# The mixture of a decoder layer: all experts on all tokens, or tokens scattered by expert through DRAM and gathered back

## The chip, the core and the metric

The kernel runs on one core of one Trainium2 chip. The metric is the device time of one execution in microseconds (us), median of several runs. The core's engines are TensorE (PE in the rows, with PEld for its weight loads), VectorE (DVE), ScalarE (ACT), GpSimd (POOL) and SyncE (SP). Sixteen DMA engines serve it.

## What is computed

Two decoder layers over x of 16 sequences, 128 tokens and 256 features, all in fp32. Each of the six sub-blocks is x + f(layernorm(x)): a recurrence, a grouped attention with a context, **the feed-forward block with a mixture of experts** (the one that is changed), a windowed attention, a cross attention and a gated feed-forward block. The changed block, shortened:

```python
dense_in = rms(h, pre1)
dense_out = rms(gelu(dense_in @ w_gate) * (dense_in @ w_up) @ w_down, post1)     # 256 -> 1024 -> 256
probs = softmax((rms(h) * router_scale * ROOT) @ router_w)                        # 8 experts
top_w, top_i = top_k(probs, 2);  top_w = top_w / sum(top_w) * per_expert_scale[top_i]
aff = zeros(T, 8).at[arange(T), top_i].set(top_w)
g, u = moe_in @ we_gate[e], moe_in @ we_up[e]                                     # moe_in = rms(h, pre2), 256 -> 128
eo = (gelu(g) * u) @ we_down[e]                                                   # 128 -> 256
moe_out = rms(sum_e(aff[e] * eo[e]), post2)
x = x + rms(dense_out + moe_out, post)
```

Each token uses 2 of 8 experts; the other six have the weight 0.

## The kernel before

The program is a row of stages, each a block in which the five engines run their own lists of instructions and meet others by semaphores; a stage begins when all engines have left the one before. `experts` (L1022) is the third stage. A `batch` below is one sequence (128 tokens on 128 partitions), a `group` is four batches (512 tokens); there are four groups.

In before, a group goes through 16 steps q. Steps 0 to 7 are slices of 128 of the dense block's 1024 hidden features, steps 8 to 15 the eight experts, each for all 512 tokens. `gate_up(g, q)` (L1177) makes two products of 512 columns, each from three terms (high*high, low*high, high*low, since a number is split into a rounded high part and a rest), 12 matmuls in all. ScalarE takes the gelu (L1245), VectorE multiplies by the other product (`hide`, L1322), ScalarE rounds the result (L1249), VectorE takes the rest (`split_hidden`, L1328), and `down(g, q)` (L1197) makes 12 matmuls of 256 columns. TensorE's order is gate_up(q), down(q-1). For an expert, `weigh` (L1355, L1357) adds its product times its share to `ex_mixture`, four instructions for four batches. `ex_share` is 0 where the token does not use the expert.

At a group's head TensorE transposes four batches (`turn`, L1152), ScalarE copies them to `ex_h_t` and rounds them to `ex_h_high`, and `route` (L1160) makes the router's logits. VectorE finds the two best experts by comparing all pairs (`choose`). During the first group ScalarE rounds all weights and GpSimd takes their rests (L1134), three tiles for each step.

After the last matmul of a group follows the tail: `square` (L1236, ScalarE) and `normalise` (L1125 and L1126, GpSimd, a power of -1/2) for each of three rms norms, and on VectorE `combine` (L1368, L1372), `scale_sum` and `add_sum` (L1379, L1386) and `measure` (L1393, the statistics of the next layernorm). In before the tails of groups 0 to 2 lie beside the steps of the next group; that of the last group has nothing beside it. GpSimd and SyncE do little in the stage; SyncE loads the next stage's four weights (5 MB) at its start. `split_keys`, `set_keys` and `fetch_keys` belong to the stage before and are not changed.

## Time and profile before

| | us |
|---|---|
| median of 3 runs | 1542.45 (1539.98 to 1542.99) |
| the profiled execution's own time | 1544.03 |
| its span in the trace | 1542.2 |
| `experts`: first matmul of group 0 | 368.73 |
| first matmul of groups 1, 2, 3 | 442.93, 515.21, 586.19 |
| last matmul ends | 656.77 |
| the next stage's first VectorE instruction | 673.64 |

Over the span PE is busy 1336.0 us (87%), PEld 1047.2, DVE 1066.6, ACT 838.5 and POOL 596.0. A timeline line says start, duration, engine, line, operation, output and inputs, count, and in brackets how long the engine sat idle before and what released it. A matmul's duration overlaps that of the next, so that the pace is read from the starts. A matmul of two fp32 operands (the router's) stands as two passes in the trace: 16 rows for 8 instructions.

### The profile page before, as it was taken

To read this page: it belongs to the slowest core of one execution; us is meant where nothing else is said; L and a number is where in the kernel's file an instruction comes from. 1 tells how busy PE (TensorE), PEld (TensorE's weight loads), DVE (VectorE), ACT (ScalarE), POOL (GpSimd) and SP (SyncE) were. 2 spreads that over 40 slices of the span, in tenths; PEclk is the share of its full clock that TensorE was granted. 3 is DMA by queue.
4 is the path that set the end of the run, shared out by engine and by line. 5 is a ranking of instruction groups with operands and counts; after the bars stand their busy time and mean duration, and the time that the engine had idled before them with its cause. 6 is when DMAs were issued, how large, how long until landed. Compare 5 with 4: busy or idle time off the path is not lost. (4 is left out here: it accounts for less than half of the span.)

```text
span 1542.2 us, 26692 instructions
## 1 busy us (share of the span) xinstructions
PE 1336.0 (87%) x8144; PEld 1047.2 (68%) x8144; DVE 1066.6 (69%) x2067; ACT 838.5 (54%) x1853; POOL 596.0 (39%) x685
## 2 busy tenths in 40 slices
PE   6994888886999999928998999899987899888998
PEld 5772555555888888816776777777766565557887
DVE  6997888893566676677777777877784566653443
ACT  5452888884543434345665666566654456552332
POOL 2003655555610000047656656656664333310000
PEclk9996999997999999968999999999999799998999
DMA  8001333313000000020000000000000000000000
GB/s 311 3 0 40 84 82 82 82 42 136 1 1 1 0 0 1 1 99 1 1 1 0 0 0 0 0 0 0 0 1 2 4 4 3 3 1 0 15 14 28
DMA packets 30739, 40.28 MB, mean 26 GB/s; under 512 B 4369, under 2 KB 25873, under 8 KB 29265
## 3 DMA queue, kind: packets, MB, share of 16 engines
q1 hardware_dynamic: 30672, 39.45, 8.4%
q8 instruction: 35, 0.57, 0.2%
q14 instruction: 32, 0.25, 0.1%
HBM read 28.96 MB, written 2.10 MB: 20 GB/s over the span
## 5 line engine op out<-in xcount | busy, mean ns | idle before, releaser
L1811 ACT ACTIVATE wi_weights<-wi_psum,wi_bias,wi_scale 128x128 f32<-128x128 f32 x256 | 113.9, 454 | 114.4 <-DVE wi_bias L1921 114.4
L1586 POOL TENSOR_TENSOR wi_straight<-wi_straight,wi_crossed 128x512 f32<-128x512 f32 x80 | 109.9, 1373 | 5.8 <-DVE wi_crossed L1907 5.7
L951 DVE TENSOR_REDUCE gq_top<-gq_psum 128x4 f32<-128x512 f32 x128 | 86.8, 678 | 28.6 <-PE gq_psum L838 27.8
L1574 POOL TENSOR_TENSOR wi_scratch<-wi_sums,wi_eps 128x4 f32<-128x4 f32 x80 | 36.2, 452 | 161.3 <-DVE wi_sums L1890 159.9
L1912 DVE TENSOR_REDUCE wi_top<-wi_psum 128x4 f32<-128x512 f32 x64 | 44.0, 688 | 75.6 <-PE wi_psum L1701 75.5
L905 ACT ACTIVATE gq_weights<-gq_weights 128x512 f32<-128x512 f32 x128 | 81.3, 635 | 22.0 <-DVE gq_weights L959 20.6
L845 PE MATMUL gq_psum<-const,gq_weights 128*128 128x128 f32 x512 | 79.2, 278 | 15.0 <-ACT gq_weights_t L911 15.0
L1125 POOL TENSOR_TENSOR ex_scratch<-ex_squares,ex_eps 128x4 f32<-128x4 f32 x12 | 2.4, 201 | 229.6 <-ACT ex_junk L1236 229.6
L1249 ACT ACTIVATE ex_hidden_high<-ex_gated 128x512 fp32r<-128x512 f32 x64 | 40.5, 633 | 92.5 <-DVE ex_gated L1322 92.5
L1322 DVE TENSOR_TENSOR ex_gated<-ex_gated,ex_psum 128x512 f32<-128x512 f32 x64 | 43.9, 686 | 64.0 <-PE ex_psum L1177 52.6
L959 DVE TENSOR_TENSOR gq_weights<-gq_psum,gq_top 128x512 f32<-128x512 f32 x128 | 87.2, 681 | 0.0
L1575 POOL TENSOR_TENSOR wi_scale<-wi_scratch,minus_half 128x4 f32<-128x4 f32 x80 | 84.6, 1057 | 6.3
L1652 PEld LDWEIGHTS wi_psum<-const,wi_straight 128*128 128x128 f32 x320 | 51.1, 174 | 50.9 <-issue 50.0
L911 ACT ACTIVATE gq_weights_t<-gq_psum 128x512 f32<-128x512 f32 x128 | 76.0, 594 | 11.8 <-PE gq_psum L845 11.0
L845 PEld LDWEIGHTS gq_psum<-const,gq_weights 128*128 128x128 f32 x512 | 62.1, 142 | 29.8 <-ACT gq_weights_t L911 16.9
L1723 PE MATMUL wi_psum<-wi_wo_high,wi_out_high 128*128 128x256 f32 x256 | 46.0, 302 | 41.7 <-DVE wi_out_low L1875 39.1
L1710 PE MATMUL wi_psum<-wi_weights_t,wi_values 128*128 128x512 f32 x128 | 78.3, 697 | 0.8 <-DVE wi_weights_t L1928 0.8
L1907 DVE TENSOR_TENSOR wi_crossed<-wi_raw,wi_sin_q 128x256 f32<-128x256 f32 x128 | 78.8, 655 | 0.0
L2335 DVE TENSOR_REDUCE cr_top<-cr_psum 128x4 f32<-128x512 f32 x64 | 43.7, 682 | 45.8 <-PE cr_psum L2150 45.8
L1245 ACT ACTIVATE ex_gated<-ex_psum 128x512 f32<-128x512 f32 x64 | 38.1, 596 | 64.0 <-PE ex_psum L1177 64.0
L1596 POOL TENSOR_TENSOR wi_weights<-wi_weights,wi_inverse 128x512 f32<-128x512 f32 x64 | 66.4, 1038 | 8.9 <-remote 4.6
L1701 PEld LDWEIGHTS wi_psum<-wi_k_t,wi_q_t 128*128 128x128 f32 x512 | 68.4, 194 | 1.7
(343 smaller groups left out, 4078.3 us busy)
## 6 DMA issues: line engine op xcount, KB each, us to landing
gq_keys<-in_ctx_keys_dram SPq DMA_DIRECT2D x16, 512.0 KB, 3.8
gq_keys_diagonal<-gq_key_parts SPq DMA_DIRECT2D x64, 128.0 KB, 3.9
x<-in_x_dram SPq DMA_DIRECT2D x4, 512.0 KB, 8.6
gate<-in_gate_dram SPq DMA_DIRECT2D x2, 1024.0 KB, 5.7
up<-in_up_dram SPq DMA_DIRECT2D x2, 1024.0 KB, 7.7
down<-in_down_dram SPq DMA_DIRECT2D x2, 1024.0 KB, 9.9
wq<-in_wq_dram SPq DMA_DIRECT2D x1, 2048.0 KB, 9.9
wo<-in_wo_dram SPq DMA_DIRECT2D x1, 2048.0 KB, 14.3
```

Source lines behind the costliest of these rows:

```text
L845: mm = pe.transpose(ps[:, bank(unit, t, u), j * P:j * P + P], weights[:, u % RINGS, j * P:j * P + P], ident)
L905: act.activation(weights[:, u % RINGS], weights[:, u % RINGS], ACT.Exp, scale=SCALE).then_inc(weighed, 1)
L911: act.activation(weights_t[:, u % PTS], ps[:, bank(unit, t, u), :], ACT.Copy).then_inc(taken, 1)
L951: dve.tensor_reduce(top[:, u % 4, :], rows(u), AX.X, ALU.max).then_inc(topped, 1)
L959: dve.tensor_tensor(weights[:, u % RINGS].rearrange("p (j t) -> p j t", t=P), rows(u), wide(top[:, u % 4, :], [P, 4, P]), ALU.subtract).th ...
L1575: found = pool.tensor_tensor(scale[:, scale_at], scratch2[:], net.half[:, 0:4], ALU.pow)
L1586: added_up = pool.tensor_tensor(straight[:, at], straight[:, at], crossed[:, at], ALU.add)
L1596: pool.tensor_tensor(weights[:, g % 2], weights[:, g % 2], wide(inverse[:, g % 2], [P, 4, P]), ALU.mult).then_inc(normalised, 1)
L1701: mm = pe.matmul(bank[:, j * P:j * P + P], q_t[:, g % 2, j, :], k_t[:, s, g, :], start=False, stop=(j == 3), skip_group_check=True)
L1710: pe.matmul(ps[:, AV, :], values[:, s, g * DH:g * DH + DH], weights_t[:, g % 2], start=True, stop=True).then_inc(attended, 1)
L1811: act.activation(weights[:, g % 2, j, :], ps[:, SC + g % 2, j * P:j * P + P], ACT.Exp, bias=bias[:, g % 2, j:j + 1], scale=scale[:, g, j:j ...
L1907: dve.tensor_tensor(crossed[:, at, :, to], raw[:, at, :, source], over_heads(sin[:, to]), ALU.mult).then_inc(parts, 1)
```

## The change

1. **The experts leave the steps.** STEPS is 8 instead of 16; a group is now only the dense block. Its result is copied out of PSUM to `ex_dense`, which now holds all 16 batches.
2. **The router is brought forward.** All 16 batches are normalised at once into `ex_y`. Batches 4 to 15 are transposed and routed in four rounds of three batches, between steps 1 to 4 of group 0. VectorE chooses for all 16 batches at once in steps 5 to 7.
3. **Places are counted.** With three small matmuls (`count`) and a scan, each (token, expert) pair gets a place in a list that is sorted by expert, each expert padded to whole blocks of 128 places. 2 x 16 x 128 pairs need at most 40 blocks (`TILES`). Indices are whole numbers in `ex_index`; `ex_owner` says whose each block is.
4. **Scatter.** GpSimd issues 32 indirect DMAs, each 128 rows of 1 KB of `ex_y` to their places in `slot_x` in DRAM. `slot_x` is cleared by one DMA of 5.2 MB in the first stage.
5. **Mixture.** Behind three dense groups (`EARLY`), 20 pairs of blocks run: SyncE fetches a pair (256 KB, 4 buffers), TensorE makes 4 transposes, loads the owners of both blocks into registers, makes 12 matmuls of 256 columns with weights addressed by these registers (gate and up side by side in one tile `egu`), 2 transposes and 6 matmuls of 256 columns; SyncE stores the pair to `slot_y` (3 buffers). All 40 blocks are always run.
6. **Gather and tail.** When all pairs are stored, GpSimd issues 32 indirect DMAs that bring back two rows for each token (`ex_first`, `ex_second`). The fourth dense group runs meanwhile, with group 0's tail in its steps 4 to 7. The tails of groups 1, 2 and 3 follow the last matmul.
7. The load of the next stage's weights is issued behind all stores. Expert weights are rounded in group 1 by ScalarE and their rests taken in group 2 by VectorE.

The core of the diff:

```diff
@block.sync
+            def fetch(k):
+                if k >= XINS:
+                    sp.wait_ge(s_turned, k - XINS + 1)
+                sp.dma_start(slot_rows[:, k % XINS], slot_block(net.slot_x, k)).then_inc(slots_in[k % XINS], 16)
+            def store(k):
+                sp.wait_ge(s_taken, k + 1)
+                sp.dma_start(slot_block(net.slot_y, k), s_out[:, k % OUTS]).then_inc(stored[k % OUTS], 16)
+            sp.wait_ge(scattered, 16 * TOP * NB)
+            for k in range(XINS):
+                fetch(k)
+            for k in range(PAIRS):
+                if k + XINS < PAIRS:
+                    fetch(k + XINS)
+                store(k)
...
             load_attn1(nc, net, ("wk", "wv", "wq", "wo"))
@block.gpsimd
+            for i in range(TOP):
+                pool.wait_ge(indexed, i + 1)
+                for b in range(NB):
+                    pool.indirect_dma_start(net.slot_x[:], bass.IndirectOffsetOnAxis(ap=index[i][:, b:b + 1], axis=0),
+                                            y[:, b, :], None).then_inc(scattered, 16)
...
+            gather(0)
+            gather(1)
+            normalise(0, 1)
+            gather(2)
+            gather(3)
+                normalise(0, 2)
+                normalise(3, 0)
...
@block.tensor
+            def mixture():
+                pe.wait_ge(owned, 1)
+                of = {}
+                for i in range(-3, PAIRS):
+                    if i + 3 < PAIRS:
+                        slot_turn(i + 3)
+                        of[i + 3] = [pe.value_load(owner[0:1, 2 * (i + 3) + j:2 * (i + 3) + j + 1],
+                                                   min_val=0, max_val=EXPERTS - 1) for j in range(2)]
+                    if 0 <= i + 2 < PAIRS:
+                        slot_gate_up(i + 2, of[i + 2])
+                    if 0 <= i + 1 < PAIRS:
+                        slot_hidden(i + 1)
+                    if i >= 0:
+                        slot_down(i, of.pop(i))
...
@block.vector
+            for g, k in left():
+                late(g, k)
+            finish(NG - 1)
             measure(NG - 1)
```

TensorE, between the dense steps and the experts: before, an expert's step stands behind the dense ones, 12 matmuls of 512 columns for gate and up and 12 of 256 (the last row is the first of these):

```order
L1177 MATMUL ex_psum<-ex_h_high,ex_egate_high 128x512 [waits ex_w_split,ex_hidden_ready]
L1177 MATMUL ex_psum<-ex_h_high,ex_egate_high 128x512
L1177 MATMUL ex_psum<-ex_h_high,ex_egate_low 128x512 x2
L1177 MATMUL ex_psum<-ex_h_low,ex_egate_high 128x512 x2
L1177 MATMUL ex_psum<-ex_h_high,ex_eup_high 128x512 x2
L1177 MATMUL ex_psum<-ex_h_high,ex_eup_low 128x512 x2
L1177 MATMUL ex_psum<-ex_h_low,ex_eup_high 128x512 x2
L1197 MATMUL ex_psum<-ex_edown_high,ex_hidden_high 128x256 [waits ex_logits_read,ex_high_ready]
```

Now a pair's iteration on TensorE begins so (ISA and REGISTER_ALU are register instructions):

```order
L1339 MATMUL ex_psum<-const,ex_slot_rows 128x128 [waits ex_s_split,ex_slots_in0]
L1339 MATMUL ex_psum<-const,ex_slot_rows 128x128 x3
L1383 TENSOR_LOAD ex_owner
L1383 ISA x2
L1383 TENSOR_LOAD ex_owner
L1383 ISA x2
L1353 ISA [waits ex_s_ready,ex_s_split]
L1353 MATMUL ex_psum<-ex_egu_high,ex_s_high 128x256
L1353 ISA
L1353 MATMUL ex_psum<-ex_egu_high,ex_s_high 128x256
L1353 REGISTER_ALU
L1353 MATMUL ex_psum<-ex_egu_low,ex_s_high 128x256
```

The expert's work moved out of the groups into iterations that start with a fetched tile and two loads to registers. On SyncE, in the middle of the mixture (nothing stood here before):

```order
L1157 DMA ex_slot_rows<-slot_x 128x2x256 [waits ex_s_turned]
L1161 DMA slot_y<-ex_s_out 128x2x256 [waits ex_s_taken]
L1157 DMA ex_slot_rows<-slot_x 128x2x256 [waits ex_s_turned]
L1161 DMA slot_y<-ex_s_out 128x2x256 [waits ex_s_taken]
L1157 DMA ex_slot_rows<-slot_x 128x2x256 [waits ex_s_turned]
```

A fetch now stands behind the store of an earlier pair. On VectorE, from the last product on: before,

```order
L1368 SCALAR_TENSOR_TENSOR ex_mixture<-ex_mixture,ex_norm,rows 128x256 [waits ex_dense_ready,ex_norm_ready]
L1368 SCALAR_TENSOR_TENSOR ex_mixture<-ex_mixture,ex_norm,rows 128x256 x3
L1372 TENSOR_TENSOR ex_mixture<-ex_mixture,ex_dense 128x256 [waits ex_own_dve]
L1372 TENSOR_TENSOR ex_mixture<-ex_mixture,ex_dense 128x256 x3
L1379 SCALAR_TENSOR_TENSOR ex_mixture<-ex_mixture,ex_norm,rows 128x256 [waits ex_norm_ready]
L1379 SCALAR_TENSOR_TENSOR ex_mixture<-ex_mixture,ex_norm,rows 128x256 x3
L1386 TENSOR_TENSOR x<-x,ex_mixture 128x256 [waits ex_own_dve]
L1386 TENSOR_TENSOR x<-x,ex_mixture 128x256 x3
```

and now, the first of three such rounds (for groups 1, 2 and 3):

```order
L1670 SCALAR_TENSOR_TENSOR ex_first<-ex_second,ex_weight,ex_first 128x256 [waits ex_scaled] x4
L1692 SCALAR_TENSOR_TENSOR ex_first<-ex_first,ex_norm,rows 128x256 [waits ex_norm2]
L1692 SCALAR_TENSOR_TENSOR ex_first<-ex_first,ex_norm,rows 128x256 x3
L1696 TENSOR_TENSOR x<-x,ex_first 128x256 [waits ex_own_dve]
L1696 TENSOR_TENSOR x<-x,ex_first 128x256 x3
L1677 SCALAR_TENSOR_TENSOR ex_first<-ex_first,ex_norm,rows 128x256 [waits ex_norm1]
L1677 SCALAR_TENSOR_TENSOR ex_first<-ex_first,ex_norm,rows 128x256 x3
L1686 TENSOR_TENSOR ex_first<-ex_first,ex_dense 128x256 [waits ex_dense_ready,ex_own_dve]
L1686 TENSOR_TENSOR ex_first<-ex_first,ex_dense 128x256 [waits ex_dense_ready] x3
L1701 BN_STATS stats<-x 128x6 [waits ex_own_dve]
L1701 BN_STATS stats<-x 128x6 x3
```

The second wait of that round, `ex_norm2`, is for a power that GpSimd takes behind all 32 gathers.

## Rows read from the trace of the kernel before

**Rows 1.** Busy time in stretches, and granted clock (PEclk)

```profile
core 0: us, PE busy (x) PEld busy (x) DVE busy (x) ACT busy (x) POOL busy (x), PEclk, DMA share, GB/s
200.00:250.00 50.00, 41.27 (x286) 26.88 (x284) 43.96 (x87) 41.91 (x79) 29.22 (x24) 1.00 0.32 80
...
368.70:442.90 74.20, 73.09 (x408) 63.79 (x409) 41.77 (x80) 37.91 (x86) 36.38 (x47) 0.96 0.01 5
442.90:514.00 71.10, 70.36 (x399) 61.50 (x399) 47.76 (x105) 29.97 (x63) 3.63 (x6) 0.98 0.00 1
...
656.80:673.60 16.80, 0.00 (x0) 0.00 (x0) 9.27 (x24) 4.08 (x16) 2.42 (x5) 0.52 0.00 0
```

**Rows 2.** Timeline of TensorE, one dense step, and the first expert's step

```profile
378.30 0.63 PE L1177 MATMUL ex_psum<-ex_h_high,ex_gate_high 128*128 128x512 f32 x2
...
381.05 0.64 PE L1197 MATMUL ex_psum<-ex_down_high,ex_hidden_high 128*128 128x256 f32 x4
...
382.48 0.63 PE L1177 MATMUL ex_psum<-ex_h_high,ex_gate_high 128*128 128x512 f32 x2
...
403.86 0.63 PE L1177 MATMUL ex_psum<-ex_h_high,ex_egate_high 128*128 128x512 f32 x2
```

**Rows 3.** Timeline of TensorE between group 0 and group 1

```profile
437.90 1.04 PE L1152 MATMUL ex_psum<-const,ex_h_tok 128*128 128x128 f32 x8
...
440.42 0.74 PE L1197 MATMUL ex_psum<-ex_edown_high,ex_hidden_low 128*128 128x256 f32 x4 [0.53 <-DVE ex_hidden_low L1328]
441.00 2.08 PE L1160 MATMUL ex_psum<-router_w,ex_h_t 128*128 128x8 f32 x16
442.93 1.20 PE L1177 MATMUL ex_psum<-ex_h_high,ex_gate_high 128*128 128x512 f32 x2
443.93 1.05 PE L1177 MATMUL ex_psum<-ex_h_high,ex_gate_low 128*128 128x512 f32 x2
```

**Rows 4.** Timeline, the tail of the last group and the next stage's start

```profile
656.80 1.66 DVE L1357 SCALAR_TENSOR_TENSOR ex_mixture<-ex_psum,ex_share,ex_mixture 128x256 f32<-128x256 f32 x4 [0.83 <-PE ex_psum L1197]
658.49 0.42 ACT L1236 ACTIVATE ex_junk<-ex_mixture 128x256 f32<-128x256 f32 x1 [4.79 <-DVE ex_mixture L1357]
...
660.12 0.42 ACT L1236 ACTIVATE ex_junk<-ex_mixture 128x256 f32<-128x256 f32 x1
...
660.98 1.01 POOL L1126 TENSOR_TENSOR ex_norm<-ex_scratch,minus_half 128x4 f32<-128x4 f32 x1
662.03 1.67 DVE L1368 SCALAR_TENSOR_TENSOR ex_mixture<-ex_mixture,ex_norm,rows 128x256 f32<-128x256 f32 x4 [3.57 <-POOL ex_norm L1126]
663.74 1.43 DVE L1372 TENSOR_TENSOR ex_mixture<-ex_mixture,ex_dense 128x256 f32<-128x256 f32 x4
...
671.91 1.41 DVE L1393 BATCH_NORM_STATS2 stats<-x 128x6 f32<-128x256 f32 x4
...
673.64 1.17 DVE L192 BATCH_NORM_AGGREGATE mean_var<-stats 128x2 f32<-128x6 f32 x16 [0.33 <-PEq L1034]
```

**Rows 5.** DMA issues (count, KB, us to landing); an issue in SyncE's timeline

```profile
out_dram<-x SPq DMA_DIRECT2D x4, 512.0 KB, 3.0
...
xwq<-in_xwq_dram SPq DMA_DIRECT2D x1, 256.0 KB, 2.9
...
675.20 0.43 SPq L186 DMA_DIRECT2D gate<-in_gate_dram  x1
```

**Rows 6.** Idle time of TensorE before line L838, in a loop (us, times)

```profile
its engine sat idle before it (us, times) until:
  issue: 14.9, 17
```

**Rows 7.** Timeline of ScalarE and of GpSimd, one line each

```profile
375.59 0.40 ACT L1228 ACTIVATE ex_gate_high<-gate 128x256 fp32r<-128x256 f32 x1
...
675.21 3.80 POOL L198 TENSOR_TENSOR rstd<-wi_scratch,minus_half 128x15 f32<-128x15 f32 x1
```

More of the change, by code:

```diff
@@ L23 @@
 F32R = mybir.dt.float32r
+I32 = mybir.dt.int32
 P = 128
@@ L1205, in one @@
+            turn(0)
+            route(0)
+            for g in range(NG):
+                if g == EARLY:
+                    mixture()
                 for q in range(STEPS):
+                    if g == 0 and 1 <= q <= 4:
+                        turn_ahead(q)
+                    if g == 1 and q == 1:
+                        count()
                     gate_up(g, q)
+                    if g == 0 and 1 <= q <= 4:
+                        route(q)
                     if q > 0:
                         down(g, q - 1)
-                if not last:
+                if g + 1 < NG:
@@ L1210, in one @@
                     turn(g + 1)
                 down(g, STEPS - 1)
-            turn(0)
-            rounds(pe, one)
         @block.scalar
@@ L1240, in one @@
+            for q in range(2):
+                round_weights(q)
+            take(0)
+            for g in range(NG):
+                if g == EARLY:
+                    square_dense(EARLY - 1)
+                    mixture()
                 for q in range(STEPS):
-                    if first and q + 2 < STEPS:
+                    if g == 0 and q + 2 < STEPS:
                         round_weights(q + 2)
+                    if g == 0 and 1 <= q <= 4:
+                        take_ahead(q)
@@ new lines, in scale_dense, with mix @@
+            def scale_dense(b, source):
+                dve.scalar_tensor_tensor(dense[:, b, :], source, norm[:, 0, b:b + 1], row("L0_ffn_rn_post1"),
+                                         ALU.mult, ALU.mult).then_inc(dense_ready, 1)
+            def mix(g):
+                for b in range(GB * g, GB * g + GB):
+                    dve.wait_ge(scaled, b + 1)
+                    dve.scalar_tensor_tensor(first[:, b, :], second[:, b, :], weight[:, 1, b:b + 1], first[:, b, :],
+                                             ALU.mult, ALU.add).then_inc(mixed, 1)
@@ L1380, in scale_sum, with finish @@
+                for b in range(GB * g, GB * g + GB):
+                    dve.wait_ge(dense_ready, b + 1)
+                    dve.tensor_tensor(first[:, b, :], first[:, b, :], dense[:, b, :], ALU.add).then_inc(summed, 1)
+            def finish(g):
+                dve.wait_ge(norm_ready[2], g + 1)
+                for b in range(GB * g, GB * g + GB):
+                    own.did(dve.scalar_tensor_tensor(first[:, b, :], first[:, b, :], norm[:, 2, b:b + 1],
                                                      row("L0_ffn_rn_post"), ALU.mult, ALU.mult))
-            def add_sum(g):
```

695 lines of the change are left out of this document (474 added, 221 removed).

## The prediction

> **What bounds the kernel now.** I read the stretches first [rows 1]: in `experts` TensorE is busy 73.1 of 74.2 us in group 0 and 70.4 of 71.1 us in group 1, at a granted clock of 0.96 and 0.98, while VectorE is busy 42 and 48 us and GpSimd 3.6 us once the weights are split. So TensorE sets the stage's length up to its last matmul at 656.8 us. Then comes the timeline of its steps [rows 2]: a step lasts 4.18 us (378.30 to 382.48), of which 2.75 us are the 12 matmuls of 512 columns and 1.43 us the 12 of 256, 0.119 us each. The eight steps of a group's experts are pure price: 32 such steps in all, 133.8 us. Last comes the tail [rows 4]: from 656.80 us to the next stage at 673.64 us TensorE does nothing (the last of rows 1 has it at 0.00 us busy), since sums, squares, powers and statistics of the last group wait for each other.
>
> The change attacks the 133.8 us and pays in three currencies: a pair's iteration that isn't purely TensorE's, GpSimd's queue, and the tail. I add up where each event falls on the trace's axis, and compare the end of the stage with 673.3 us (the last statistics, 671.91 + 1.41) [rows 4].
>
> **Three dense groups.** The eight dense steps of group 0 have run at 403.86 us but for the last down product [rows 2]. The router's four rounds come in between: each 6 transposes (1.04/8 = 0.13 each, 0.78 us) and 12 passes of 8 columns (16 took 1.93 us from 441.00 to 442.93, so 1.45 us) [rows 3], together 4 x 2.23 = 8.9 us: 412.8. A group's boundary takes 5.03 us now (437.90 to 442.93); without the router's 1.93 us it is 3.1 [rows 3]. The copy to `ex_h_t` goes too, so nothing new is late there. Group 1 is 8 x 2.75 + 7 x 1.43 = 32.0 and 0.6 for the counting matmuls: 412.8 + 3.1 + 32.6 = 448.5. Group 2: 451.6 to 483.6, and its last transposes and down product 2.7: 486.3. VectorE's choosing (all 16 batches, 1024 elements an instruction) and ScalarE's rounding of expert weights come in single steps near 4 us; I add 1.7 us for where they stick out. **488 us.** The half-speed matmuls after two boundaries (two in about 1.05 us instead of 0.62 [rows 3]) may go; I count no gain.
>
> **Scatter.** Indices are there at about 426 us. GpSimd's price for one indirect DMA, c, stands in no row. The bounds are SyncE's issue, 0.43 us [rows 5], and GpSimd's dearest small instruction, 3.80 us [rows 7]. I take **c = 1.1 us**, near its power of 128x4, 1.01 us [rows 4], as the nearest thing that it does in software for 128 partitions. 32 x 1.1 = 35 us, so all is scattered by 465 us: hidden behind groups 1 and 2. The cover lasts up to c = 1.8. Clearing `slot_x` lies in the first stage, behind the loads; a longer `const` costs 0.3 us.
>
> **Fill.** When TensorE has finished group 2, ScalarE still has to copy the dense result (two of about 0.55) and square four batches (0.54 each [rows 4], 2.2 us), before it rounds the first pair; with VectorE's rest the first gate product starts 4.9 us late. Then three overlapping first iterations, about 11 us: first pair out at **504 us**, a fill of 16.
>
> **A pair's pace, T.** TensorE's own work W: 6 transposes 0.8, 12 matmuls of 256 columns 1.4, 6 more 0.7: 2.9 us. Register instructions between the matmuls (about ten) 0.5. Two register loads from `ex_owner` with their checks: no row shows one. The lower bound is 0; the upper is twice the wait for the engine's own sequencer at a loop's turn, 14.9/17 = 0.88 us [rows 6], 1.8; I take the middle, 1.0. W = 4.4. The other bound is the ring through SyncE: the fetch for iteration k+2 is issued behind the store of pair k. From the last matmul of pair k: ScalarE's copy 0.7, store issue 0.43, fetch issue and landing 2.9 (256 KB [rows 5]) and 0.6 behind the store's bytes, 4.7 us in all = L. Two iterations take at least L + W, so T = (4.7 + 4.4)/2 = 4.55. ScalarE (0.6 + 0.4 + 0.4 + 0.6, a 256-column one being 0.40 [rows 7]) and VectorE (1.8) are below it. I take **T = 4.5**: 19 x 4.5, less 7 since the last three iterations lack transposes, loads and gates: 504 + 78.5 = **582.5 us**. With W = 2.9 and L = 4.0, T is 3.4; with W at 5.7 or more T is W.
>
> The Trainium skill ("DMA: Bandwidth & Descriptors", Latency and other measured facts) puts the floor of a register load (`tensor_load`) at about 600 ns. By it the two cost 1.2 instead of 1.0 us and the pace is 4.65, the end 3 us later; no run so far shows one.
>
> **Fourth group and gather.** 8 x 4.18 and 1.2 for the last chain: TensorE ends at 582.5 + 34.6 = **617.1**. GpSimd starts to gather 3.7 us after the last pair (copy, store, landing). It must do groups 0 and 1 (16c), wait for group 0's squares (about 28 us after the last pair), take a power (1.3), do 16 more and another power: `ex_norm2` comes at max(3.7 + 16c, 28) + 2.6 + 16c = 48 us after the last pair, 630.6.
>
> **The tail.** Only there can VectorE start its first `finish`. What follows is three rounds of mix 1.66, finish 1.67 + 1.43, combine 1.67 + 1.43 and measure 1.41 [rows 4], 9.3 us each, plus 1.7 for the last group's dense scaling, and a last chain of squares (4 x 0.54), power and waits of 4.4: 34 us. 630.6 + 34 = **664.6** against 673.3; with the 0.3 the sum is -8.4 us. The tail behind the last matmul grows from 16.6 to 47 us: of 133.8 us saved, about 94 go to the mixture, 9 to transposes and counting, 31 to the tail. From the profiled execution's 1544.0 this gives 1535.6; the median of the runs shown is 1.6 below that, so I forecast **1534 us**.
>
> **Rivals.**
> *Pairs at full pace.* Register loads run behind transposes already queued, fetches land in time: T = 3.4, 21 us less: 1513. For it: TensorE is 83% busy in the attention at clock 1.00 [rows 1] with many register instructions. Against it: the ring through SyncE has hardly any slack.
> *GpSimd is the bound: slower than before.* If c = 2.0, the 32 gathers last 64 us, `ex_norm2` comes 70 us after the last pair instead of 48, and the scatter ends late enough to start the mixture about 5 us later: 1534 + 22 + 5 = 1561. The point from which it decides is c = 1.55, where the 8.4 us are spent. For it: the place of each gather on one queue, ahead of two powers that VectorE waits for. Against it: GpSimd's other small work is near 1 us.
> The Trainium skill (same page, Anatomy of one DMA, GpSimd path) fits 2.0 us + bytes/436 GB/s to one such DMA, 2.3 us for these; it also says that most of this is the landing, not the building. If GpSimd paid it all each time, this rival would hold; if only landing, c is below it. No row here decides.
> *Slow pairs: slower too.* A pair's iteration has about 2 us without matmuls in one piece. After 0.53 us of idle and the thin router matmuls the trace has TensorE at 1.2 instead of 2.4 GHz: two matmuls in 1.05 instead of 0.62 us, for some 2.7 us [rows 3]. If that comes in most iterations, or a load costs 1.8, T is 5.8: 1534 + 25 = 1559.
> *The change does less than it says.* All 40 blocks run whatever the tokens choose, so no imbalance can hurt or help; I see no chance worth a number.
>
> **Chances.** The forecast 0.40 (1524 to 1544), full pace 0.17, GpSimd bound 0.20, slow pairs 0.20, something small that I have not seen 0.03. Faster than before by over 0.2% (3.1 us, about what can be told from no change): 0.17 and most of the forecast's, 0.50. Within: 0.11. Slower: 0.39. Both signs hold much of it: the likeliest case's own range is 1524 to 1544; the whole, with c from 0.9 to 2.1 and T from 3.4 to 5.9, is 1508 to 1566.
>
> **What would show it.** Right: first pair out near 504 us; pairs every 4.5 us with TensorE's wait in front of the transposes, released by the fetch's DMA; scatter done long before 488; the last matmul near 617, then 47 us of idle TensorE in which VectorE's first long wait is for `ex_norm`, released by GpSimd. Wrong: a scatter that the mixture waits for, or an `ex_norm` later than 70 us after the last pair (c); a wait at the gate products behind the loads, or a clock below 0.8 in the mixture (T); a dense group longer than 36 us, where choosing or rounding did not fit beside the steps.

## The result, and the profile after

The changed kernel took **1579.4 us** (median of 4; 1573.9 to 1582.1) against 1541.2 of the kernel before: a ratio of 1.024, interval 1.021 to 1.028. The forecast was 1534, its range ended at 1566. The profiled execution has a span of 1580.1 us.

The stretches of the changed kernel, where [rows 1] show the kernel before (same columns). Cut at: behind the choosing, the scatter's second half, group 2, the mixture from its first transposes to its last matmul, the fourth group, the tail.

```profile
413.50:450.00 36.50, 32.81 (x176) 26.75 (x174) 16.77 (x46) 16.78 (x35) 16.89 (x18) 1.00 0.15 52
450.00:483.00 33.00, 12.05 (x39) 9.21 (x40) 3.96 (x6) 4.09 (x8) 16.15 (x17) 0.54 0.31 103
483.00:515.80 32.80, 32.80 (x195) 29.15 (x194) 17.85 (x28) 12.56 (x26) 1.24 (x2) 1.00 0.00 0
515.80:614.30 98.50, 74.87 (x483) 70.34 (x482) 35.89 (x75) 39.28 (x90) 1.21 (x2) 0.84 0.30 92
614.30:661.00 46.70, 36.37 (x192) 31.29 (x190) 15.45 (x28) 15.28 (x36) 22.27 (x24) 0.89 0.49 182
661.00:714.00 53.00, 0.02 (x1) 0.00 (x0) 33.41 (x88) 19.08 (x70) 20.29 (x27) 0.53 0.10 29
```

The second line is the one to stop at. A stretch of purely dense steps, in which TensorE should be busy all the time, has it busy 12 of 33 us, VectorE 4 and ScalarE 4. Only GpSimd is at work as planned, on the scatter, with an indirect DMA every 1.26 us. The timeline of that stretch (start, duration; in brackets the idle time before, and what ended it):

```profile
458.68 0.96 POOL L1219 DMA_INDIRECT slot_x<-ex_y,ex_index  x1 [0.30 <-issue]
...
459.76 0.37 PE L1264 MATMUL ex_psum<-const,ex_y 128*128 128x128 f32 x1 [0.82 <-issue]
...
461.18 0.37 PE L1264 MATMUL ex_psum<-const,ex_y 128*128 128x128 f32 x1 [1.04 <-issue]
...
464.67 0.37 PE L1264 MATMUL ex_psum<-const,ex_y 128*128 128x128 f32 x1 [2.33 <-issue]
...
470.06 0.96 POOL L1219 DMA_INDIRECT slot_x<-ex_y,ex_index  x1 [0.30 <-issue]
...
471.69 0.37 PE L1264 MATMUL ex_psum<-const,ex_y 128*128 128x128 f32 x1 [2.43 <-issue]
472.55 1.93 SPq L1157 DMA_DIRECT2D ex_slot_rows<-slot_x  x4
475.26 0.60 ACT L1523 ACTIVATE ex_gated<-ex_psum 128x512 f32<-128x512 f32 x1 [19.71 <-remote]
```

The eight transposes (L1264) wait on nothing between themselves and take 1.04 us together in [rows 3]; here they come one by one over 12 us, and the idle time before each is put to "issue": no semaphore that the profile shows was awaited. ScalarE sits 19.71 us before a GELU whose input was long there (TensorE's last gate or up product before it ended at 449.6; "remote" means that no releaser was found). It starts again 5 us after the last scatter. A second such stall lies beside the gathers: the fourth group lasts 46.7 us. I call both **the stall** from here on.

The tail answers to [rows 4]: the last statistics end at 713.4 (673.3 before), TensorE is idle for the 53 us of the last stretch.

### The profile page after: what moved, and what is told of

Same layout as the page of the kernel before. It is cut to its first block and busy times, and to the rows that moved or that the text cites. A ratio compares the mean times of both kernels' runs of the same rounds, so it can differ in the third digit from the quotient of the medians.

```text
span 1580.1 us, 26270 instructions
## 1 busy us (share of the span) xinstructions
PE 1275.1 (81%) x7839; PEld 1003.8 (64%) x7886; DVE 1009.7 (64%) x1953; ACT 834.1 (53%) x1872; POOL 639.2 (40%) x724
## 5 line engine op out<-in xcount | busy, mean ns | idle before, releaser
L1641 DVE TENSOR_TENSOR ex_gated<-ex_gated,ex_psum 128x512 f32<-128x512 f32 x32 | 22.0, 686 | 94.7 <-PE ex_psum L1312 41.0
L2010 PEld LDWEIGHTS wi_psum<-const,wi_straight 128*128 128x128 f32 x320 | 43.6, 154 | 48.8 <-issue 48.0
L2059 PE MATMUL wi_psum<-wi_k_t,wi_q_t 128*128 128x128 f32 x512 | 68.0, 276 | 3.7 <-ACT wi_q_t L2160 1.4
L2448 POOL TENSOR_TENSOR cr_keys_diagonal<-cr_qk,const 128x256 f32<-128x256 f32 x32 | 19.4, 626 | 112.3 <-ACT cr_qk L2620 112.3
L2141 ACT ACTIVATE wi_raw<-wi_psum 128x512 f32<-128x512 f32 x80 | 47.8, 597 | 31.6 <-PE wi_psum L2046 31.0
```

The source lines that it names most:

```text
L2059: mm = pe.matmul(bank[:, j * P:j * P + P], q_t[:, g % 2, j, :], k_t[:, s, g, :], start=False, stop=(j == 3), skip_group_check=True)
```

## The experiments

They ran in seven comparisons, each on one chip, with its own runs of the kernel before (medians 1540.6 to 1541.5 in all, so that one is the same everywhere). Eight of the eighteen runs have a single execution each (in the order below the 1st, 2nd, 4th, 5th, 6th, 10th, 13th and 16th).

**First comparison (chip 15): is it the scatter, and what about it?**

Without the scatter:

```
-            for i in range(TOP):
-                pool.wait_ge(indexed, i + 1)
-                for b in range(NB):
-                    pool.indirect_dma_start(net.slot_x[:], ...)
...
-            sp.wait_ge(scattered, 16 * TOP * NB)
```

> The changed kernel without its 32 scatters (the mixture then multiplies rows of zeros, and the gathered rows are not the tokens' results); nothing else differs. In the changed kernel TensorE is busy for 12 of the 33 us from 450 to 483, group 2's first gate product is at 480.0 and the mixture's first transpose at 515.8, where the steps of 4.18 us would have given 488. Theory A (the stall from 445 to 477 comes from the scatters): it is gone, and the mixture's first transpose is at 486 to 491; the span is some 25 to 30 us shorter, near 1552. Theory B (the stall comes from the dense groups themselves, for instance the count matmuls and the expert weights' rounding that the change put into group 1): the first transpose stays at 510 to 516 and the span near 1580.

1546.7 us. The same bytes by SyncE:

```
+                for b in range(NB):
+                    sp.dma_start(net.slot_x[P * (NB * i + b):P * (NB * i + b + 1), :],
+                                 y[:, b, :]).then_inc(scattered, 16)
```

> The changed kernel with the 32 scatters of GpSimd replaced by 32 plain copies of SyncE, each of the same 128 KB from ex_y to 128 rows of slot_x in a row, issued at the same moment (the rows do not stand by expert, so the output is not the reference's). The same 4.2 MB pass, by the hardware's queue. Theory A1 (GpSimd's software queue, or its making of descriptors, is what stops the other engines): no stall, the mixture's first transpose at 486 to 491 and a span near 1552. Theory A2 (the bytes and packets themselves, 1 KB rows written to DRAM beside the instruction fetches): the stall stays, at most shorter as the copies take less than the scatters' 41 us; first transpose at 500 to 516.

1545.5 us. In both the stall before the mixture is gone; the copies move 4.2 MB and cost TensorE nothing. The stretch 450 to 483 of the second (the longer lead, run beside it on this chip, has TensorE busy for 10.46 of the same 33 us):

```profile
450.00:483.00 33.00, 33.00 (x191) 29.07 (x190) 17.20 (x27) 12.77 (x27) 1.21 (x2) 1.00 0.03 11
```

Theories A and A1 hold in kind: it is the indirect DMAs, not the bytes, nor what else the change put into the groups. In size both ran a little ahead of them: the mixture's first transpose is at 485.4 and 484.1 (486 to 491 were expected), the spans are 1544.8 and 1543.7 (1552). The gathers are left in both, and so is the fourth group's stall: 43 us from the last pair to the last matmul.

The order in SyncE's queue:

```
-            for k in range(XINS):
+            for k in range(XINS + 2):
                 fetch(k)
             for k in range(PAIRS):
-                if k + XINS < PAIRS:
-                    fetch(k + XINS)
+                if k + XINS + 2 < PAIRS:
+                    fetch(k + XINS + 2)
                 store(k)
```

> The changed kernel; SyncE's queue in the mixture issues fetches 0 to 5 and then fetch k+6, store k, where it had fetches 0 to 3 and then fetch k+4, store k. In the changed kernel pairs come in twos, 10.1 us for two (one of 2.8 us, one of 7.2), and TensorE waits 11.0 us in 8 places on a fetch, with 1.1 us more for the registers behind each. Theory C (the fetch k+5 stands behind store k in SyncE's queue, so that it is issued only one pair before it is needed): the waits on fetches go, no pair takes over 4 us, the 85.7 us from the first pair's last matmul to the last pair's fall to 55 to 65, and the span by 20 to 30 us to 1550 to 1560. Theory D (the pace is set by TensorE's clock and the engines' hand-overs, the fetch only fills a gap): 78 to 85 us, span over 1570.

1553.4 us, ratio 1.008 (1.006 to 1.009), 26 us less than the changed kernel. Theory C holds: no wait on a fetch is left, the stores stand 3.1 to 3.3 us apart, and from the first pair's last matmul to the last pair's it is 57 us instead of 85.7. The lines of the same order on another chip are in the section on the steps.

88 indirect DMAs that nobody reads, added to the kernel before:

```
+                    pool.indirect_dma_start(net.spare[:], bass.IndirectOffsetOnAxis(ap=mine[:, b:b + 1], axis=0),
+                                            net.rows[:, 0:D], None).then_inc(burst_done, 16)
...
+                    if n == 0:
+                        burst(32 if g < NG - 1 else 24)
```

> The kernel before with 88 indirect DMAs of GpSimd added in its expert stage, each of 128 rows of 1 KB from the table of row vectors to a spare DRAM tensor that nobody reads (the output stays the reference's): 32 behind the first norm of round 1 (from 485 us, of which to 512 in the first pass of the loop), 32 behind that of round 2 (from 556, to 583 in the loop's second pass, in which the kernel before has no record of an instruction fetch), 24 behind that of round 3 (from 628, straight code). GpSimd's rounds are written out, the other engines' loop stays. Theory T1 (the engines starve for instructions, whose fetches are held up while the software queue works): TensorE loses 10 us or more in the bursts of rounds 1 and 3, and under 2 us in the 28 us of the second burst that lie in the loop's second pass. Theory T2 (the software DMAs stop the engines in another way, looped or not): all three bursts lose alike, 0.4 to 0.7 us for each us of a burst. If there is no loss in any: the stall needs something of the changed kernel, such as its scattered targets or its straight groups.

1626.4 us: 85 us lost to DMAs without a reader. The bursts themselves last from 485.3 to 526.7, 586.7 to 627.0 and 690.2 to 721.7. The stretches around them:

```profile
485.00:540.00 55.00, 30.88 (x141) 25.42 (x141) 18.36 (x41) 7.27 (x12) 32.02 (x33) 0.75 0.22 77
586.00:635.00 49.00, 21.41 (x104) 17.95 (x103) 13.68 (x29) 4.81 (x8) 31.40 (x33) 0.71 0.25 86
690.00:735.00 45.00, 31.60 (x159) 26.73 (x157) 20.19 (x44) 7.90 (x13) 24.47 (x25) 0.85 0.20 71
```

All three lose, the second too, which lies in the loop's second pass: TensorE is not busy for 24.1, 27.6 and 13.4 us of the stretches, 0.58, 0.68 and 0.43 for each us of a burst, which is about what theory T2 said (0.4 to 0.7). The DMA view of 550 to 650 us, packets by queue:

```profile
DMA packets 1536, 4.20 MB, mean 42 GB/s; under 512 B 512, under 2 KB 512, under 8 KB 1536
## 3 DMA queue, kind: packets, MB, share of 16 engines
q0 software_dynamic: 1536, 4.20, 12.1%
```

The queues "instruction", which have 4 and 3 packets in the 110 us before, have no line here: no engine fetched code by a recorded DMA while 27 us were lost. That is against theory T1. It was my first one, since "issue" without a semaphore looks like missing instructions.

**Second (chip 9): which kind of DMA?** The same bursts with other contents, and the weights' load moved.

> The kernel before with three bursts of GpSimd DMAs that nobody reads, behind the same norms as in the run with 88 indirect ones (output stays the reference's). There the engines ran on for some 12 us of each burst and then all but stopped until some 6 us after its end, also in the loop's second pass without a record of an instruction fetch: the fetch theory fell, and the open question is what about a GpSimd DMA does it. Burst 1: 32 plain (not indirect) DMAs of 128 KB. Burst 2: 32 indirect ones with rows of 64 B in place of 1 KB (128 rows each). Burst 3: 24 indirect ones of 1 KB rows, with a wait for all landed after each 8. Theory G (GpSimd's making of descriptors for a row each, whatever their bytes): burst 1 loses under 3 us, burst 2 as before (20 to 27 us in 40), burst 3 as before. Theory H (bytes through the software queue: a queue that fills up): burst 1 and the full rows lose, burst 2 under 3 us; burst 3 with its pauses loses under half of what it lost. Theory I (any GpSimd DMA): bursts 1 and 2 both lose over 15 us. For pauses: if what builds up in the first 12 us drains in a pause of 2 to 4 us, burst 3 loses under 5 us.

> As the run above with other bursts. Burst 1: 16 indirect DMAs of 128 rows of 1 KB, with a power of 1.0 us on GpSimd behind each (a pitch of some 2.3 us, so half the rate). Burst 2: 32 indirect DMAs of 64 rows (half the rows and bytes each). Burst 3: 24 of 128 rows with a wait for all landed after each 4. Theory R (what counts is the rate of rows: above some rate a backlog grows): burst 1 and burst 2 lose under 3 us each, burst 3 under 5. Theory N (what counts is the number of rows since the start, 1300 to 1500 in the 12 us that pass before the engines stop, whatever the pace): burst 1 loses from its 11th or 12th DMA on, burst 2 from the 22nd or so, each 8 us or more, and burst 3 from its 11th.

```
             sp.wait_ge(turned, NG)
+            for g in range(NG):
+                sp.wait_ge(gathered[g], 16 * TOP * GB)
             load_attn1(nc, net, ("wk", "wv", "wq", "wo"))
```

> The changed kernel with the longer lead of the fetches in SyncE's queue (53 us ... 1553 us as measured with that alone), and with the next stage's 5 MB of weights loaded only behind the last gather, where they were loaded beside the first ones. Theory S (the gathers alone stop the engines in the fourth group, as the scatters did in the third): TensorE loses the same 10 to 14 us in the fourth group, last matmul and span move by under 3 us, 1550 to 1557. Theory L (the load is what the gathers collide with): the loss in the fourth group is under 3 us, and the span some 8 us shorter, near 1545. A cost of its own is possible where the weights come too late for the next stage: they take 18 us, and 40 us lie between the last gather and their first use.

1547.8, 1551.1 and 1510.0 us (the last is the middle of three executions, 1509.9 to 1515.1; a fourth took 3067 us, and with it the median is the 1512.6 that later texts compare with). (In the third text "53 us ..." is a slip; 1553 is meant.) Neither theory S nor L had foreseen the third: in it TensorE was busy all 33 us from 450 to 483, with the scatter as before. The code ahead of that stretch had not changed. So nothing may be concluded from these three before it is known whether this chip has the stall at all.

**Third (chip 9 again): kernel or chip?**

> The changed kernel as it is, once more, beside the next three. In the run with the late load the scatters' stall was gone (TensorE busy for 33.0 of the 33 us from 450 to 483, against 10.5 in the run that has only the longer lead), although nothing before 590 us differs but four waits of SyncE. Those two ran on different chips. Theory P (the chip, or its state at the time, decides whether GpSimd's indirect DMAs stop the other engines): the four kernels of this comparison behave alike, all with the stall (then this one near 1579) or none (then near 1579 - 28 - 12 = 1539 to 1548). Theory Q (the program's layout decides): this one is at 1575 to 1583 as before, and the late load again near 1512.

> The longer lead of the fetches and the late load, once more. Theory P: near 1512 if the changed kernel beside it comes to 1539 to 1548, and 1545 to 1557 if that one stays near 1579. Theory Q: 1508 to 1516 beside a changed kernel of 1575 to 1583.

> The kernel before with the 88 indirect DMAs in three bursts, once more (1626 us and 85 us lost the first time). Theory P: over 1600 if the changed kernel beside it has its stall, else 1545 to 1552 as the two runs with other kinds of bursts had (which ran on the other chip). Theory Q: over 1600 whatever the others do.

```
             sp.wait_ge(turned, NG)
+            for g in range(NG):
+                sp.wait_ge(turned, NG)
             load_attn1(nc, net, ("wk", "wv", "wq", "wo"))
```

> The changed kernel with four waits of SyncE more, each already fulfilled when it is reached, at the place where the late load has its four; they cost under 0.5 us. Theory P: as the changed kernel beside it, within 5 us. Theory Q (layout): it may lose the stall and be 25 to 40 us shorter than the changed kernel beside it.

1539.4, 1511.1, 1542.6 and 1540.5 us. The **unchanged text of the changed kernel** takes 1539.4 us here, ratio 0.999 (0.998 to 1.000), and the bursts cost 1 us instead of 85. Theory P holds, Q falls: the program's text does not decide. The same scatter on this chip (its 32 DMAs take 43.5 us here and 41.3 with the stall):

```profile
450.00:483.00 33.00, 33.00 (x190) 29.08 (x190) 17.27 (x27) 12.78 (x27) 18.75 (x19) 1.00 0.30 102
```

**Fourth (chip 7): the chip or the occasion, and the kind once more.**

> The longer lead and the late load, in a third comparison, to see whether GpSimd's indirect DMAs stop the other engines here. Theory P (the chip decides): on a chip that has shown no stall it is near 1512 with TensorE busy for 33 of the 33 us from 450 to 483; on one that has shown it, it is at 1540 to 1560 with TensorE busy for under 15 of the 33. Theory O (it is the occasion, not the chip): either, on either.

> The kernel before with bursts of three kinds (32 plain copies of 128 KB by GpSimd; 32 indirect DMAs of 128 rows of 64 B; 24 of 128 rows of 1 KB, a wait for all landed after each 8), once more, beside the run with the late load. If that one has its stall here, this tells which kind does it. Theory G (a descriptor for each row): bursts 2 and 3 lose 10 us or more each, burst 1 under 3. Theory H (bytes through the software queue): 1 and 3, not 2. Theory I (any DMA of GpSimd): 1, 2 and 3. If there is no stall in the run beside it: near 1548 as the first time, and nothing is told apart.

1551.0 and 1580.8 us: this chip has the stall, TensorE is busy for 10.49 of the 33 us. That fits theory P, but it doesn't refute theory O: chip 7 was had once, and no chip with the stall was had twice. The three kinds of burst can be read. Burst 1 (plain), burst 2 (rows of 64 B) and burst 3 (full rows, a pause after each 8), here:

```profile
485.00:510.00 25.00, 24.32 (x150) 21.65 (x148) 18.15 (x37) 8.38 (x15) 14.06 (x27) 1.00 0.45 150
556.00:610.00 54.00, 25.70 (x117) 21.57 (x116) 14.39 (x30) 6.13 (x10) 30.10 (x31) 0.68 0.04 5
662.00:700.00 38.00, 28.56 (x165) 24.63 (x164) 24.32 (x53) 9.94 (x21) 25.91 (x27) 0.96 0.24 84
```

and the same kernel on chip 9:

```profile
485.00:510.00 25.00, 25.00 (x146) 22.05 (x145) 19.10 (x40) 7.33 (x12) 17.26 (x32) 1.00 0.51 169
556.00:610.00 54.00, 53.22 (x302) 46.42 (x302) 36.96 (x81) 22.26 (x45) 35.09 (x34) 0.97 0.04 6
628.00:667.00 39.00, 27.92 (x164) 24.37 (x162) 26.33 (x58) 10.08 (x22) 25.07 (x27) 0.88 0.24 82
```

Beside 32 plain copies by GpSimd at 150 GB/s TensorE is busy 0.7 us less than on chip 9; beside 32 indirect DMAs of hardly any bytes (5 GB/s) it is busy 27.5 us less, and GpSimd's next power comes 35 us later after the burst's start. **None of the three theories comes true whole**: H and I fall with bursts 2 and 1, and G, which had it right for those two, wanted 10 us or more from burst 3 as well. That burst has 28.56 us busy of 38, on chip 9 27.92 of 39 (the stage's own end lies in both), and the stage's end comes at most 2 us later for it.

So what counts is that the DMAs are indirect, not their bytes. That it is the number of rows isn't shown: a plain copy here moves 128 rows of 1 KB too, and the DMA view has the same 1536 packets for the 32 plain ones as for 32 indirect ones of full rows. One caution: the plain burst lasts 17.4 us (481.7 to 499.1), so that only its last 5 us lie behind the 12 us after which the indirect bursts begin to stall.

The 24 without a pause, third burst of the 88, had lost 13 of 45. The burst with pauses never has more than 8 in a row, some 10 us. Either something builds up within 12 us and drains in a pause of 2, or nothing ever gets that far; the two aren't told apart, and the comparison is one between chips 7 and 15.

**Fifth (chip 10) and sixth and seventh (chip 3): does a pause cure it?**

```
+                    if b % 8 == 7:
+                        pool.wait_ge(scattered, 16 * (NB * i + b + 1))
...
+                pool.wait_ge(gathered[g], 16 * TOP * GB)
```

> The longer lead and the late load, and with them a wait of GpSimd for all landed after each 8 indirect DMAs, among the scatters and among the gathers. Without these waits this kernel took 1511 to 1513 us in two comparisons without the stall and 1551 in one with it. In the bursts on a chip with the stall (chip 7), 32 indirect DMAs without a pause lost some 27 us, 24 with a pause after each 8 (1.7 and 2.6 us long) lost 1.4. Theory D (a backlog of rows' descriptors that a pause lets drain): 1510 to 1522 wherever it runs, TensorE busy for 31 or more of the 33 us from 450 to 483; the three pauses put the end of the scatter from 471 to 477 to 481, still ahead of the mixture's start at 484. Theory E (the last burst was spared for another reason, being the shortest and followed by the tail): with the stall 1540 or more.

> The changed kernel with the same pauses of GpSimd and nothing else. It took 1579 with the stall and 1539 without. Theory D: 1537 to 1546 wherever it runs. Theory E: 1565 or more with the stall.

> The kernel before with three bursts of indirect DMAs that nobody reads: 16 of 128 rows of 1 KB with a power of 1.0 us on GpSimd behind each (pitch 2.4 us, 53 rows per us); 32 of 64 rows (pitch 1.2, 52 rows per us); 24 of 128 rows without a pause (pitch 1.26, 102 rows per us). The last is the marker: with the stall it loses 10 us or more, without it under 2, and then nothing is told apart. Theory R (a rate of rows above which a backlog grows): bursts 1 and 2 lose under 3 us each. Theory N (a number of rows since the last pause, 1000 to 1500): bursts 1 and 2 lose 8 us or more each, from some 25 us after their start. Theory M (a number of DMAs, 10 or so, whatever their rows): burst 2 loses from 12 us after its start, burst 1 from 24.

> The longer lead, the late load, and the pauses after each 8 among the scatters alone; the gathers, 16 in a row in the fourth group, go without, and tell by themselves whether the chip has the stall (there the fourth group of the kernel without pauses took some 12 us more than without the stall). Without the stall anywhere: 1512 to 1518. With it in the gathers: Theory D (the pauses drain what builds up) TensorE is busy for 31 or more of the 33 us from 450 to 483, and the kernel takes 1522 to 1535, where without pauses it took 1551; Theory E (pauses do nothing for the scatter) under 15 of the 33, and 1550 to 1558.

> The same kernel (pauses among the scatters alone, the longer lead, the late load) in a new comparison, since the last one fell on a chip (3) without the stall. Where the fourth group shows no loss (its last hidden step some 29 us behind the first gather): 1510 to 1516, nothing told apart. Where it does (39 us behind): Theory D, TensorE busy for 31 or more of the 33 us from 450 to 483 and 1522 to 1535 in all; Theory E, under 15 of the 33 and 1550 to 1558.

1519.7, 1547.3, 1542.6, 1512.4 and 1510.1 us. None of the three comparisons fell on a chip with the stall: the marker burst, and the fourth groups, show no loss. So they tell only prices, and theories D, E, R, N and M all stay untested. The pauses among the gathers cost 8 us (1547.3 against 1539.4, 1519.7 against 1511.1); those among the scatters nothing that can be told (1510.1 and 1512.4 against 1511.1), since groups 1 and 2 cover them. **Whether pauses take the stall out of the changed kernel stays open**, as does what the rate and number of rows do (the bursts of the second and fifth comparison).

The same kernels on both kinds of chip, in us:

| kernel | chip 9 | with the stall | difference |
|---|---|---|---|
| changed | 1539.4 | 1579.4 (chip not noted) | 40.0 |
| longer lead, late load | 1511.1 | 1551.0 (chip 7) | 39.9 |
| before, 88 indirect DMAs | 1542.6 | 1626.4 (chip 15) | 83.8 |
| before, three kinds of burst | 1547.8 | 1580.8 (chip 7) | 33.0 |

But for the one of 3067 us, the executions of a kernel agree within a comparison (1551.4 to 1555.9 on chip 15, 1535.7 to 1542.0 in ten on chip 9).

**Chip, occasion or recording?** Chip 9 had no stall in two comparisons and chip 3 none in two; chips 15 and 7 had it in the one comparison that each was in. So it goes with the comparison; that it goes with the chip and not with its state at the time is the likelier reading, not a shown one. And there is a rival that no run settles. The two kinds of trace differ in something else. The DMA view's line of the scatters, with the stall and on chip 9 (the last number is the median time to landing):

```profile
slot_x<-ex_y,ex_index POOLq DMA_INDIRECT x32
...
slot_x<-ex_y,ex_index POOLq DMA_INDIRECT x32, 2.4
```

Where there is the stall the view finds no landing for any of GpSimd's DMAs, and most of the records of the indirect ones' semaphores are missing: 98 of the scatters' 512 increments are in the trace (32 DMAs x 16), all 512 on chip 9. It is so in each trace from chips 15 and 7, from the first DMA on. On chip 7 the 32 plain copies have all their 512 records, the 32 indirect DMAs of 64 B rows 101, and the 24 with pauses, which stall next to nothing, 143 of 384. On chips 9, 10 and 3 hardly any is missing (the most is 7 of 1152). Every execution reported here has a span and a clock, and those come from its recording. Whether the stall would be there in an execution that nobody records, or comes of what the recording does with these DMAs, isn't shown.

## Why the prediction was wrong, step by step

Two executions of the same code are at hand, so each step can be held against the one without the stall (chip 9, span 1533.8) and against the one with it. Its stretches, from the mixture on:

```profile
484.00:578.50 94.50, 72.53 (x485) 67.27 (x484) 35.82 (x76) 39.30 (x90) 1.21 (x2) 0.87 0.32 96
578.50:615.10 36.60, 33.92 (x193) 29.53 (x192) 15.65 (x28) 15.49 (x37) 23.13 (x24) 0.99 0.64 233
615.10:669.00 53.90, 0.00 (x0) 0.00 (x0) 34.06 (x98) 19.60 (x71) 20.45 (x30) 0.50 0.09 27
```

| step | predicted | without the stall | with it |
|---|---|---|---|
| mixture's first transposes | 488 | 484.1 | 515.8 |
| one indirect DMA, c (mean of the 32 scatters) | 1.1 | 1.26 (1.36) | 1.26 (1.29) |
| first pair out | 504 | 498 | 528 |
| last pair out | 582.5 | 578.3 | 614.0 |
| last matmul | 617.1 | 615.1 | 661.0 |
| first `finish` behind `ex_norm2` | 630.6 | 629.4 | 675.5 |
| last statistics end | 664.6 | 667.4 | 713.4 |

**The step that failed** is the scatter's "hidden behind groups 1 and 2". It asked only whether the scatter is done in time, and it is (at 471 with the stall and 472 without, against 488; the forecast said by 465, though its own 426 + 35 make 461). It put at nothing what a GpSimd at work costs the others. In the execution with the stall 32 us go there (the mixture starts at 515.8 instead of 484.1), 10 in the fourth group beside the gathers (47.0 from the last pair against 36.8) and 4 in the mixture, where no indirect DMA runs: there TensorE waits 11.0 us for fetches instead of 9.1, and the rest isn't explained. The tail has none (52.4 us against 52.3); there VectorE and ScalarE wait for GpSimd anyway. That sum is 46 for these two executions and 40 for the medians. No rival named it: "GpSimd is the bound" spoke of GpSimd's own queue and would have decided from c = 1.55; c is 1.26, and `ex_norm2` came 51 us after the last pair (61 with the stall), not 70. Nor could the kernel before show it, which has no indirect DMA. And the forecast would have held had the run fallen on chip 9: 1539.4 lies in its range (with 1.8 us of the 7 us gained). Which of the two the first run would fall on was chance, for which the forecast had no term.

**The groups** came 4 us earlier than forecast without the stall. Group 0 with the router's rounds was through at 409.3 instead of 412.8, group 1 gave back 2.3 (34.9 us instead of 32.6, with a wait of 1.3 for `ex_h_low`), the boundary between groups 1 and 2 took 2.3 instead of 3.1, and of the 1.7 us for what sticks out nothing showed but that wait.

**The pace was right by luck, two errors that cancel.** 498 to 578.3 gives, by the prediction's own formula, (80.3 + 7)/19 = 4.6 against 4.5. But W is not 4.4. SyncE's timeline on chip 9, a store and the fetch behind it:

```profile
507.48 0.36 SPq L1161 DMA_DIRECT2D slot_y<-ex_s_out  x1
507.88 0.47 SPq L1157 DMA_DIRECT2D ex_slot_rows<-slot_x  x1
510.79 0.36 SPq L1161 DMA_DIRECT2D slot_y<-ex_s_out  x1
511.19 0.47 SPq L1157 DMA_DIRECT2D ex_slot_rows<-slot_x  x1
516.68 0.36 SPq L1161 DMA_DIRECT2D slot_y<-ex_s_out  x1
517.09 0.47 SPq L1157 DMA_DIRECT2D ex_slot_rows<-slot_x  x1
519.86 0.36 SPq L1161 DMA_DIRECT2D slot_y<-ex_s_out  x1
```

Stores come 3.3, 5.9 and 3.2 us apart: every second pair waits for its fetch. The mechanism (two iterations last L + W) is the predicted one; the waits stand where they were forecast, in front of the transposes. TensorE's waits in the mixture on chip 9 (us in total, times, longest):

```profile
PE ex_psum L1339 <- DMA ex_slot_rows<-slot_x: 9.1, 8, 2.0
PE ex_psum L1353 <- issue: 8.8, 9, 1.2
PE ex_psum L1353 <- DVE ex_s_low L1717: 3.8, 1, 3.8
```

With the longer lead (chip 9) the stores are evenly apart:

```profile
507.93 0.36 SPq L1161 DMA_DIRECT2D slot_y<-ex_s_out  x1
508.33 0.47 SPq L1157 DMA_DIRECT2D ex_slot_rows<-slot_x  x1
511.21 0.36 SPq L1161 DMA_DIRECT2D slot_y<-ex_s_out  x1
511.61 0.68 SPq L1157 DMA_DIRECT2D ex_slot_rows<-slot_x  x1
514.41 0.36 SPq L1161 DMA_DIRECT2D slot_y<-ex_s_out  x1
```

and the two waits of its matmuls are

```profile
PE ex_psum L1355 <- DVE ex_s_low L1719: 3.8, 1, 3.8
PE ex_psum L1355 <- issue: 1.9, 9, 0.3
```

So W is 3.3 us, registers included, not 4.4: the register loads run behind transposes that are already queued, as the first rival had it, and their 1.0 us shows only where TensorE has waited for a fetch first, as the "issue" before the gate products (L1353), some 1.1 us in each of eight pairs. L was sized too short in return: two iterations last 9.2 us by that formula (9.4 by the stores from 499.0 to 569.8), which leaves 5.9 to 6.1 for L, against 4.7. (The prediction's "with W at 5.7 or more T is W" is a slip besides: its two bounds cross where W is L, 4.7.) The rival "pairs at full pace" was right about W and wrong about the ring; with the ring mended it is what happens: the mixture lasts 70 instead of 94 us, at a granted clock of 0.98 instead of 0.87:

```profile
484.00:554.50 70.50, 64.00 (x489) 59.52 (x488) 36.01 (x76) 38.24 (x91) 1.21 (x2) 0.98 0.41 128
```

The trace of chip 9 has the forty loads too (TENSOR_LOAD, L1383): 0.30 us each in the median, 0.63 at most, and 0.15 and 0.02 for the two register instructions behind each. Two make 0.94 us, near the 1.0 of the forecast and the 1.1 exposed; the size was right, and only that it adds to W was wrong.

The Trainium skill's floor of a register load ("DMA: Bandwidth & Descriptors", Latency and other measured facts, about 600 ns) would make 1.2 us of the two. The trace's 0.30 us for one is below it, and here the trace decides; with a full queue the exposed part falls to 0.2 us, at nine of twenty pairs.

**Fourth group and tail.** 36.8 instead of 34.6 for the group, beside the gathers and a load; with the load moved away it is 34.9 on the same chip. The norm's formula with c = 1.26 gives 51 us and the trace has 51.1; VectorE waits for it as forecast:

```profile
629.42 1.67 DVE L1692 SCALAR_TENSOR_TENSOR ex_first<-ex_first,ex_norm,rows 128x256 f32<-128x256 f32 x4 [10.18 <-POOL ex_norm L1190]
```

What follows lasts 38 us, not 34, the term mis-sized by 4: the later powers too come late (idle times of 0.6 and 2.3 us before `finish` and `combine`, "<-POOL ex_norm").

Summed up, without the stall the stage ends 5.9 us earlier than before where 8.7 were forecast, and the median is 1.8 us lower where 7 were. There the forecast's path is the one that the trace shows, with W and L mis-sized against each other and the tail by 4 us, and the change is worth next to nothing even so (the ratio's interval ends at 1.000): of the 134 us of expert steps 94 go to the mixture, and some 24 of those to the fetch that stands behind a store. Those 24 us are the waits, the registers exposed behind them and the lower clock together. With the stall the change loses 38.

**A kernel that is faster where there is no stall.** Longer lead and late load: 1511.1 us on chip 9, ratio 0.981 (0.979 to 0.983). On chip 7 it takes 1551.0, ratio 1.007 (1.004 to 1.011), and loses to the kernel before. With pauses among the scatters 1510.1 and 1512.4 on chip 3. Of the late load alone there is no run, but the fourth group can be read by itself, from the last pair to the last matmul: without the stall 36.8 us with the load beside it and 34.9 without, with the stall 44.7 (chip 15) and 45.0 (chip 7). Theory L, which had the gathers collide with the load, falls; S holds, the gathers alone make the fourth group's stall.

## What to carry to other kernels

Ask of work that is moved to an idle engine not only whether it is done in time but what it does to the engines beside it: an idle span of all other engines at once, put to "issue" or "remote", is the sign. A single order of issues (a fetch that stands behind a store which waits for the end of the pipeline) cost 24 us; read the queue's timeline for steps that come in twos. And when a difference comes from a run on another chip, run the unchanged kernel there too before explaining it.

## What the runs showed of the hardware

- One text takes 1539.4 us in one comparison and 1579.4 in another. In those on chips 15 and 7 bursts of more than about ten of GpSimd's indirect DMAs of 128 rows, 1.26 us apart, all but stop TensorE, VectorE and ScalarE (TensorE busy 10 to 12 of 33 us), from 12 to 15 us after the start to some 5 us after the end, in every execution; in those on 9, 10 and 3 they don't. The kernel before takes the same 1541 us in all.
- It needs indirect DMAs, not bytes (5 GB/s are enough), and not DMAs of GpSimd as such (17 us of plain ones at 150 GB/s cost 0.7). No fetch of instructions was recorded in one of the stalls. What differs between the chips or occasions, what the engines lack, and whether the recording has a part in it, is not known.
- The Trainium skill ("DMA: Bandwidth & Descriptors", same section as above) gives, as a guess at why two of the DMA engines are slower than the others, that all DMA engines' reading of the software queue's descriptor rings in SBUF loads some of its ports. It says nothing of stopped compute engines, and no run here shows a ring or a port. The plain copies, which go through the same queue and stall nothing, speak against it as the cause here.
- One indirect DMA of 128 rows costs GpSimd mostly 0.96 us and 0.30 us of issue, for 1 KB rows in either direction (1.24 to 1.36 us in the mean of a row of them), and a wait for all landed 1.7 us.
- A register load from SBUF takes 0.30 us in TensorE's queue (median of 40) and is hidden where work is queued ahead of it.
- One of four executions of the late load on chip 9 took 3067 us. It did not come again in the 19 later ones of that kernel and its kin with pauses, and is not explained.
